# A gate's chain of small vector operations cut into five pieces and spread over four units

## What is computed

```python
x = x + ssm(cond(x))          # cond: x @ W + a rank 16 adapter chosen per batch row
                              # ssm: h = dA_t*h + dBx_t over 64 steps, y = sum_n h*C_t + D*x
y = x @ base_weight.T + base_bias + adapter2(x)     # adapter chosen per batch row
logits = y @ router_w.T                             # 4 experts
gates = softmax(logits kept at the top 2 of 4, -inf elsewhere)
mid = einsum('tf,erf->ter', y, A)                   # 4 experts x rank 16
x = x + einsum('te,teo->to', gates, einsum('ter,eor->teo', mid, B) * 4)
```

## Time and profile before

| | us |
|---|---|
| median of 3 runs | 968.85 (967.85 to 970.72) |
| the profiled execution | 977.12 |
| its span, first to last instruction | 975.2 |
| busy in the span: PE, DVE, ACT, POOL | 875.0, 766.6, 699.7, 728.5 |
| the small gate instructions, one each of 13 in a group | 0.155 to 0.291 |

### The profile page before, as it was taken

The page is one execution under the profiler, slowest core; times in us unless marked ns, Lnnn a source line. Parts: engine busy times, 40 slices in busy tenths (PEclk is TensorE's granted clock), DMA queues, the critical chain, the costliest instruction groups (busy, mean ns, idle before and its releaser), DMA issues.

```text
span 975.2 us, 19502 instructions
## 1 busy us (share of the span) xinstructions
PE 875.0 (90%) x6712; PEld 783.3 (80%) x6712; DVE 766.6 (79%) x613; ACT 699.7 (72%) x1594; POOL 728.5 (75%) x407
## 2 busy tenths in 40 slices
PE   3599799999998999889998899889998999888885
PEld 2484699889978998789878899789987998677772
DVE  2223777898889879897889978897889978898992
ACT  3225766888778877778777777687778877789850
POOL 1001687799778988788778888688788988899891
PEclk9899799999999999999999999999999999999997
DMA  8686466245442555255442455254442533131011
GB/s 178 199 319 253 114 196 184 98 166 166 119 147 86 183 145 162 67 184 147 123 148 97 149 147 149 97 184 141 122 150 72 179 106 90 34 104 34 28 39 43
DMA packets 126862, 130.34 MB, mean 134 GB/s; under 512 B 81065, under 2 KB 105641, under 8 KB 118574
## 3 DMA queue, kind: packets, MB, share of 16 engines
q1 hardware_dynamic: 119150, 121.76, 39.8%
q10 hardware_dynamic: 7616, 7.34, 2.4%
HBM read 112.16 MB, written 16.91 MB: 132 GB/s over the span
## 4 chain that ended last, share of the span: by engine, by line
PE 64%; POOL 11%; DVE 7%; issue 7%; ACT 5%; SPq 3%; DMA 2%; POOLq 0%; DVEq 0%; ACTq 0%
PE jb L900 27%; PE yp L1060 17%; POOL hC L499 9%; PE dBx L900 9%; PE yp L904 4%; DVE h L872 3%; PE yp L900 3%; PE jb L904 3%; ACT dA L545 2%; DMA W_scratch<-Wst 2%; DVE Bd L728 2%; PE yp L1065 1%; ACT stacked L571 1%; POOL HL L482 1%; SPq L293 1%
## 5 line engine op out<-in xcount | busy, mean ns | idle before, releaser
L499 POOL TENSOR_TENSOR hC<-h,Cb 128x1024 f32<-128x1024 f32 x256 | 617.2, 2419 | 102.9 <-DVE h L872 99.5
L872 DVE TENSOR_TENSOR_SCAN h<-dA,dBx 128x1024 f32<-128x1024 f32 x256 | 582.7, 2280 | 100.3 <-PE dBx L900 71.6
L545 ACT ACTIVATE dA<-dt,negA 128x252 f32<-128x252 f32 x1024 | 424.7, 494 | 9.3 <-DVE h L872 9.0
L1060 PE MATMUL yp<-ident,hC 128*128 128x128 f32 x2048 | 269.9, 275 | 10.1 <-DVE Bhl L807 4.5
L900 PE MATMUL jb<-xT,Wst 128*128 128x256 f32 x1536 | 233.8, 295 | 12.7 <-DVE Wst L842 10.7
L1060 PEld LDWEIGHTS yp<-ident,hC 128*128 128x128 f32 x2048 | 233.3, 142 | 12.6 <-POOL hC L499 7.8
L900 PEld LDWEIGHTS jb<-xT,Wst 128*128 128x128 f32 x1536 | 199.6, 193 | 20.4 <-issue 14.9
L900 PE MATMUL dBx<-Bd,stacked 96*128 96x256 f32 x1024 | 184.9, 303 | 28.0 <-ACT stacked L571 9.4
L900 PEld LDWEIGHTS dBx<-Bd,stacked 96*128 96x128 f32 x1024 | 143.5, 192 | 42.4 <-issue 40.1
L571 ACT ACTIVATE stacked<-yp 96x512 fp32r<-96x512 f32 x111 | 65.6, 591 | 115.6 <-PE yp L904 115.4
L478 POOL TENSOR_TENSOR dtx<-dt,u 128x256 f32<-128x256 f32 x64 | 55.6, 869 | 85.0 <-DVE dt L714 76.4
(11 more groups left out here) (131 smaller groups left out, 706.9 us busy)
## 6 DMA issues: line engine op xcount, KB each, us to landing
Wst<-W_scratch SPq DMA_DIRECT2D x56, 1024.0 KB, 5.1
Cb<-c_scratch SPq DMA_DIRECT2D x32, 512.0 KB, 5.1
W_scratch<-Wst SPq DMA_DIRECT2D x8, 1024.0 KB, 6.2
xres<-in_x SPq DMA_DIRECT2D x64, 128.0 KB, 4.2
out<-obuf SPq DMA_DIRECT2D x32, 256.0 KB, 2.0
xin<-in_x ACTq DMA_DIRECT2D x28, 256.0 KB, 5.4
GB<-in_L_cond_lora_B SPq DMA_DIRECT2D x64, 64.0 KB, 2.0
Cb<-in_L_cond_W SPq DMA_DIRECT2D x2, 1024.0 KB, 5.5
```

Of the source, the lines that this page charges most:

```text
L499: pool.tensor_tensor(hC[:, un % NHC, :].rearrange("p (n b t) -> p b n t", n=HS, b=2), h[:, un % NH, :].rearrange("p (b n t) -> p b n t", n ...
L545: act.activation(dA[:, half % NDA, :].rearrange("p (b n t) -> p b n t", b=GB_, n=HS)[:, :, n, 1:STEPS], dt[:, j % NDT, :].rearrange("p (b ...
L872: dve.tensor_tensor_scan(h[:, un % NH, :], dA[:, half % NDA, UNIT * p:UNIT * (p + 1)], dBx[un % 2][:, :], 0.0, ALU.mult, ALU.add).then_inc ...
L1060: last = pe.matmul(y, hC[:, un % NHC, P * n:P * (n + 1)], ident[:, :], is_transpose=True, start=un == 0 and n == 0, stop=False, skip_group ...
```

## The change

The gate's chain becomes five pieces. Piece 0 (three instructions) stays with `mid2` in unit 14. `rank` 0 (three) goes to unit 15, `rank` 1 (two) and `gate` 0 (three) to unit 16, and `gate` 1 (the last small one, and `gmT`) to unit 17, each on DVE behind the scan of its unit. DVE waits ahead of an instruction only where it reads what a former one wrote, or at the start of a piece: two waits between neighbours that don't depend on each other are gone. The instructions are the same. `gm` moves from unit 16 to unit 17, where it is the unit's last job, and to bank Y; `out` 0 and 1 move to units 18 and 19, `out` 0 from bank Y to B. `out` 2 and 3 stay.

```diff
-OF_PREVIOUS = {"x1T", "FB", "A2T", "mid", "h2T", "mid2", "gate", "gm", "out"}
+OF_PREVIOUS = {"x1T", "FB", "A2T", "mid", "h2T", "mid2", "rank", "gate", "gm", "out"}
...
-    (3, 2): [job("cond", 5, "A", (3, 5)), job("mid2", 0, "B"), job("gate", 0, None)],
-    (3, 3): [job("cond", 5, "A", (5, 8))],
-    (4, 0): [stack(10), job("gm", 0, "B"), job("cond", 6, "A", (0, 2)), stack(11)],
-    (4, 1): [job("cond", 6, "A", (2, 5)), job("out", 0, "Y")],
-    (4, 2): [job("out", 1, "B"), job("GAs", 0, None), job("cond", 6, "A", (5, 6))],
-    (4, 3): [job("cond", 6, "A", (6, 8)), job("cond", 7, "A", (0, 1))],
+    (3, 2): [job("cond", 5, "A", (3, 5)), job("mid2", 0, "B")],
+    (3, 3): [job("rank", 0, None), job("cond", 5, "A", (5, 8))],
+    (4, 0): [stack(10), job("rank", 1, None), job("gate", 0, None), job("cond", 6, "A", (0, 2)), stack(11)],
+    (4, 1): [job("gate", 1, None), job("cond", 6, "A", (2, 5)), job("gm", 0, "Y")],
+    (4, 2): [job("out", 0, "B"), job("GAs", 0, None), job("cond", 6, "A", (5, 6))],
+    (4, 3): [job("out", 1, "B"), job("cond", 6, "A", (6, 8)), job("cond", 7, "A", (0, 1))],
...
-            def gating(g, second, psum):
-
-                n = 8 if second else 0
+            def gating(g, piece, psum):
+
+                n = (0, 3, 6, 8, 11)[piece]
 
                 def link(ins):
                     nonlocal n
                     n += 1
                     ins.then_inc(gate_step, 1)
+
+                def linked():
                     dve.wait_ge(gate_step, GATE_STEPS * g + n)
...
+                if piece:
+                    linked()
+                if piece == 0:
                     top = gate[:, 2, 0:TT]
                     link(dve.tensor_reduce(top, logits, AX.X, ALU.max))
+                    linked()
                     link(dve.tensor_tensor(te(0), logits, top.unsqueeze(2).to_broadcast(shape), ALU.subtract))
                     link(dve.tensor_copy(te(5), logits))
-                    other, own = logits.unsqueeze(2).to_broadcast(pairs), te(5).unsqueeze(3).to_broadcast(pairs)
+                elif piece == 1:
                     link(dve.tensor_tensor(eq, other, own, ALU.is_equal))
+                    link(dve.tensor_tensor(gt, other, own, ALU.is_gt))
+                    linked()
                     link(dve.tensor_tensor(ee(1), eq, before[:, :, :].unsqueeze(1).to_broadcast(pairs), ALU.mult))
...
+                else:
+                    link(dve.scalar_tensor_tensor(te(4), by_expert, LORA2_SCALE,
+                                                  gate[:, 2, 0:TT].unsqueeze(2).to_broadcast(shape), ALU.mult, ALU.mult))
+                    linked()
...
-            job("gate", 0, G, G % 2, jb[0])
+            for i in range(2):
+                job("rank", i, G, G % 2, jb[0])
+            for i in range(2):
+                job("gate", i, G, G % 2, jb[0])
```

More of the change, by code:

```diff
@@ L552, in job @@
                     return softplus_parts(K // 2 * g + i, i, psum)
-                if name in ("xr", "mid", "gate", "out"):
+                if name in ("xr", "mid", "rank", "gate", "out"):
                     return
@@ L753, in gating @@
                 rank, chosen = kept[:, 64:72], kept[:, 72:80]
-                if not second:
-                    logits = mids[:, :, EM:EM + E]
+                logits = mids[:, :, EM:EM + E]
+                other, own = logits.unsqueeze(2).to_broadcast(pairs), te(5).unsqueeze(3).to_broadcast(pairs)
+                by_expert = chosen.rearrange("p (a e) -> p a e", a=TT)
+                if piece:
+                    linked()
+                if piece == 0:
                     top = gate[:, 2, 0:TT]
@@ L762, in gating @@
                     link(dve.tensor_tensor(ee(1), eq, before[:, :, :].unsqueeze(1).to_broadcast(pairs), ALU.mult))
-                    link(dve.tensor_tensor(gt, other, own, ALU.is_gt))
+                elif piece == 2:
                     link(dve.tensor_tensor(ee(0), gt, ee(1), ALU.add))
+                    linked()
                     link(dve.tensor_reduce(rank, beats[:, 0, :].rearrange("p (a e) -> p a e", e=E), AX.X, ALU.add))
-                    assert n == 8
-                    return
@@ L768, in gating @@
[L768 to L779, removed]
+                elif piece == 3:
+                    dve.wait_ge(gate_exp, g + 1)
+                    link(dve.scalar_tensor_tensor(chosen, rank, 1.5, gate[:, 1, :], ALU.is_lt, ALU.mult))
+                    linked()
+                    link(dve.tensor_reduce(gate[:, 3, 0:TT], by_expert, AX.X, ALU.add))
+                    linked()
+                    link(dve.reciprocal(gate[:, 2, 0:TT], gate[:, 3, 0:TT]))
+                else:
+                    link(dve.scalar_tensor_tensor(te(4), by_expert, LORA2_SCALE,
+                                                  gate[:, 2, 0:TT].unsqueeze(2).to_broadcast(shape), ALU.mult, ALU.mult))
+                    linked()
+                    of = [P, TT, E, R]
+                    dve.tensor_tensor(gmT[:, :, :].rearrange("p a (e r) -> p a e r", e=E),
+                                      mids[:, :, 0:EM].rearrange("p a (e r) -> p a e r", e=E),
+                                      te(4).unsqueeze(3).to_broadcast(of), ALU.mult).then_inc(gated, 1)
@@ L781, in job @@
+                assert n == (3, 6, 8, 11, 12)[piece]
             def job(name, i, g, gpar, psum):
-                if name == "gate":
-                    return gating(g, True, jb[1] if psum is None else psum)
+                if name in ("rank", "gate"):
+                    return gating(g, i + (1 if name == "rank" else 3), jb[1] if psum is None else psum)
                 if name == "GAs":
@@ L814, in job @@
                     dve.wait_ge(full["mid"], g + 1)
-                    gating(g, False, psum)
+                    gating(g, 0, psum)
                 elif name == "out":
@@ L921, in job @@
                            "h2T": (h2_masked, g + 1), "gm": (gated, g + 1)}.get(name, ())
-                if name in ("gate", "GAs"):
+                if name in ("rank", "gate", "GAs"):
                     return
```

## The result

The changed kernel takes 979.88 us (977.17 to 980.93, 4 runs) against 969.39 (967.85 to 970.72, 4 runs) of the kernel before: ratio 1.0095, 95% interval 1.0067 to 1.0122. It is slower by about 1%. The forecast was 978.5, range 974 to 983. The profiled execution of the changed kernel took 980.26 us.

The account below looks back on a forecast made before the run. PE alone was taken to set the pace of units 14 to 22. Middle groups +9.6, last group +0.3 and dropped waits -0.2 made +9.7 us: 968.85 + 9.7 = 978.5 us, range 974 to 983.

Parts of the forecast that it names:

- The burst is hidden in the middle groups: Gate instructions in unit 14: taking 2.13 us off DVE there gains PE nothing, its own work covers them.
- Rival A: Burst on PE's path after all, at the `dBx` of unit 17: faster, 960 to 966 us; chance 0.06.
- The wait at `gm`: Unit 17 of each middle group: PE waits for `gmT` behind scan 17; 1.6 us taken, 9.6 us in six groups.
- the walk: Start times reckoned step by step on DVE and PE, scan 15 to the `dBx` of unit 18: PE loses 1.65 us.
- The bound of 1.4: Low end of PE's loss in us ahead of the `dBx` of unit 18, if the dropped waits save their 0.24.
- "What moves with it, at no cost": `out` 0 and 1, ACT's copy and stores come later at no cost; smallest margin 0.8 us, bank B at `out` 1.
- It stays lost: Behind unit 18 of middle groups: no reserve takes up PE's lag, so the 1.6 us moves everything after it.
- Rival B: A reserve from unit 25 on hides most of PE's lag: +0 to +2.5 us, about 970; chance 0.12.
- The last group: The 2.1 us that DVE gains are lost in the wait at `gm`, up to scan 18: +0.3 us.
- Rival C: PE's granted clock falls behind the new gap of about 1.6 us in middle groups: 989 us; chance 0.07.
- The two waits dropped: Gate after the loop, where DVE is alone on the path: 0 to 0.24 us saved, 0.2 taken.
- The profiled execution: Its 977.12 us gave 986.8 for the changed kernel; its 8.3 us over the runs' median was carried over unchanged.

Follow-up runs that it names:

- the second comparison: The changed kernel, unedited, run and profiled once more beside the kernel before: 985.31 us against 978.85, ratio 1.0079.
- the last experiment: Middle groups as in the kernel before but two waits fewer; last group with pieces in units 14 to 16, `gm` in 17: ratio 0.9978 against the kernel before.
- four more steps: The changed kernel with the gate's last small step done five times instead of once, ahead of `gmT`: 1013.64 us in a single run.

## Why the prediction was right, and where it wasn't

**The direction and the sum** were right: +9.7 forecast, +9.7 in the first profile's distances without the disturbances, +10.5 between the medians. That the sums agree so closely is luck. The middle groups gave 7.3 us, not 9.6; the last gave 1.1, not 0.3; and the fall of the clock in one profile added the 1.6 that closed the gap. The program is 8.1 us longer, and in the second comparison 6.5 between the medians. So here is each term.

**The burst is hidden in the middle groups.** Shown, twice. Taking 2.1 us out of unit 14 brought nothing in unit 15 or 16 of any column of the table, and the last experiment, with the whole chain in unit 14, has the 106.95 us of before. Rival A is refuted.

**The wait at `gm`.** The mechanism is shown from three sides: the row with its releaser, the 1.00 us that go when gate 1 stands a unit earlier, and the one to one price of four more steps. Its size was too high: 1.65 by the walk, 1.0 measured. The steps that failed are small ones of the walk. The first piece and the residual took 0.68 us to scan 15, not 0.64 + 0.33; piece 1 let scan 16 start 0.50 after it began (372.14 to 372.64), not 0.64; pieces 2 and 3 took 0.95, not 1.07; and from the end of `gmT` to the next `dBx` it was 0.30 (378.46 to 378.76), not 0.45. I had put a full 0.213 on each instruction, and for an instruction that isn't held by the one before it is less than half of that: L766 starts 0.08 us behind L765. That rate was in the earlier trace rows, and I used it for the tail only. The bound of 1.4 that I gave below was too narrow for the same reason.

**"What moves with it, at no cost"** is the step that failed. It cost 0.2 us in each group, which I had at nothing, and its smallest margin, bank B at `out` 1, was real: it fails as soon as DVE is late, and costs 1.0 us in unit 19 where only `gm` was moved (4.92, against 2.85 and the 1.05 of `out` 1). Of those 1.0 us 0.76 are the wait. The 0.2 us are about one half `gm`'s and one half an `out`'s by the table; their cause is open.

**It stays lost.** Right. The lag at unit 20 is 1.19 us and at the next group's unit 10 it is 1.19 still; each unit in between has its old length. Rival B is refuted.

**The last group** was the worst term: +0.3 forecast, +1.1 and, where the clock fell, +2.7 measured. The walk itself held: from the gate to scan 18 it was 10.58 us in the second profile of after, against 11.01 before. What failed is that I stopped there. By scan 21 DVE has lost this again (19.00 both), and at scan 24 it is 1.3 late, where it waits 1.01 us for ACT's decays, with the same step in all kernels that have this form of the last group; I had not followed ACT. And I looked for the gap of PE in the middle groups, where it is 0.82 us, not here, where PE has nothing else to do and it is 2.9.

**Rival C,** the clock, didn't happen behind the new gaps of the middle groups: not behind 0.82 us (24 times, in the four profiles with the changed kernel's middle groups) nor behind 1.63 (six times, with four more steps). It happened in the last group, behind 2.92 us of idle time and not behind 2.88. My reason against it, that the clock stayed behind 1.71 us in the earlier trace rows, was one execution's luck: behind the same idle time ahead of `h2T`, 1.69 to 1.72 us, it fell in four profiles and stayed in seven, and behind the 1.8 us of group 3 it fell in seven of 13. In the first units of the last group it even fell with no idle time over 1.21 us in the 5 us before. The Trainium skill, "TensorE: Matmul & The Clock Gate", section "HAM oscillation — how this bites in real kernels", has idle gaps of PE as the cause, where they are long enough. The trace agrees that idle time stands ahead of the falls in the middle groups, but here the length alone doesn't decide: the clock fell or stayed behind the same gap.

**The two waits dropped** gave 0.26 us in the gate after the loop (2.55 from its first instruction to `gmT` before, 2.29 after, in all kernels that have the new form and no more steps), 0.2 forecast. The Trainium skill, "VectorE: DVE Perf Modes", section "The DRAIN you can't avoid", has it that semaphores between vector operations cost nothing; by that rule it would have been 0, and the trace doesn't agree: L766 follows L765 at 0.08 us, where a held one follows at 0.20. The same section also says that an operation which isn't held starts earlier, and with that the trace agrees.

**The profiled execution.** I carried its 8.3 us over the median as if they were spread over everything, and wrote that the middle groups repeat. They don't: it is three slow `Bd` operations, worth 11.5 us with what the clock lost behind two of them. It did no harm to a sum of differences, but a forecast of 986.8 us for the next profile missed (980.26), and whoever compares the two spans would have seen a loss of 3 us.

## What to carry to other kernels

Before breaking up a burst on one engine, look whether the bounding engine ever waits for it; two buffers can hide it whole, and then the cut can only lose. What decides is where the last piece lands against the first instruction that needs it: a queue in order holds everything behind that wait, and one unit more or less was worth 1 us in each group here. Moving the consumer later instead spends another margin (a bank that is not free yet). And where executions differ by random events, here a slow operation and a fall of the clock, compare undisturbed periods of the loop, not spans.

## What the runs showed of the hardware

- DVE's 96x1024 `Bd` operation in unit 1 takes 1.75 to 1.83 us or 4.84 to 4.89 us, with nothing in between, from execution to execution of the same program.
- The same idle time of PE is followed by a fall of the granted clock in one execution and not in another: 1.8 us in 7 of 13 profiles, 1.7 us in 4 of 11, 2.2 to 2.7 us behind a slow `Bd` in 17 of 23 cases, 2.9 us in one of two (there 0.56 and 0.59 in the two stretches of 2 us behind it). It never did behind 0.82 us (24 cases) or 1.63 (6).
- What one such fall costs depends on the place: 1.3 us behind a slow `Bd`, 1.0 to 1.3 in unit 29, 1.6 behind the last `gm`, up to 3.5 in the loop's tail.
- Two small DVE instructions that don't wait for each other start 0.08 us apart; with a wait between them 0.20.
- The distance from the `dBx` of one unit to that of the next, where the jobs are the same, is the same to 0.05 us in all undisturbed groups of all kernels, on four chips. That makes differences of 0.1 us in a program of 970 us readable.
